# Last feed-forward layer of a two-layer model: merges one block sooner, last group finished in two halves

## The reference

```
x = _layernorm(x + L1_attn(x))            # its output product and gates: "merge" below
# L1_ffn, the last feed-forward part; K0, K1, K2 are matrices of +1 and -1
h = concat([x, -x])                       # 256 features
h = 2 * relu(s0 * h @ K0)                 # 512
h = 2 * relu(s1 * h @ K1)                 # 512
y = s2 * h @ K2                           # 128
out = _layernorm(x + y)                   # (x - mean) / sqrt(var + 1e-5), per row of 128
```

## Time and profile before

| | before |
|---|---|
| device time, three runs | 624.46, 609.24, 624.79 us; median 624.46 |
| profiled execution | 602.81 us, of which the span of the core's instructions is 601.1 |
| granted TensorE clock, mean | 0.986 of 2.4 GHz |
| TensorE busy (products) | 546.1 us, 91% of the span |
| VectorE, ScalarE, GpSimd busy | 407.1, 324.2, 174.4 us |
| last layer | from about 531 us to the end |

### The profile page before, as it was taken

One profiled execution on the slowest core, in us unless ns is written; L12 is line 12 of the kernel. 1 busy time (PEld: TensorE's weight loads), 2 busy tenths in 40 slices (PEclk: granted clock), 3 DMA queues, 4 the chain that ended last, 5 costly groups with the idle time before them and its releaser, 6 DMA issues.

```text
span 601.1 us, 17481 instructions
## 1 busy us (share of the span) xinstructions
PE 546.1 (91%) x7472; PEld 373.3 (62%) x7472; DVE 407.1 (68%) x773; ACT 324.2 (54%) x574; POOL 174.4 (29%) x333
## 2 busy tenths in 40 slices
PE   4799999999999999999999996996999779897993
PEld 2445555555555557777777785774667667565672
DVE  5697999999999826263545337345899871576774
ACT  2327888788888876655555645556422330125441
POOL 7000111445535422010101006246982560010101
PEclk9899999999999999999999999898999999999998
DMA  4778667374240000001000000021673300000011
GB/s 118 153 224 212 190 149 147 81 154 79 57 104 7 5 2 2 0 7 31 1 2 1 0 1 0 2 36 39 124 93 73 73 4 4 5 1 1 1 36 35
DMA packets 54051, 33.82 MB, mean 56 GB/s; under 512 B 38853, under 2 KB 45509, under 8 KB 53974
## 3 DMA queue, kind: packets, MB, share of 16 engines
q1 hardware_dynamic: 48822, 31.65, 23.8%
q10 hardware_dynamic: 5152, 1.05, 1.1%
HBM read 20.83 MB, written 9.44 MB: 50 GB/s over the span
## 4 chain that ended last, share of the span: by engine, by line
PE 70%; DVE 13%; ACT 6%; DMA 6%; issue 2%; SPq 1%; POOL 1%; POOLq 0%; ACTq 0%; DVEq 0%
PE ps L1760 10%; PE ps L1745 9%; PE ps L1512 7%; PE ps L1514 6%; PE ps L1513 6%; PE ps L1860 6%; DMA qst<-shift_sb 4%; PE ps L1724 3%; PE ps L1933 2%; PE ps L2065 2%; DVE filtered L1344 2%; PE ps L2066 2%; ACT prob L682 2%; PE ps L1926 2%; PE ps L1602 1%
## 5 line engine op out<-in xcount | busy, mean ns | idle before, releaser
L1203 DVE TENSOR_REDUCE nmx<-ps 128x1 f32<-128x1024 f32 x128 | 154.1, 1218 | 16.6 <-PE ps L1725 15.2
L682 ACT ACTIVATE prob<-ps 128x512 f32<-128x512 f32 x256 | 137.4, 597 | 26.6 <-PE ps L1745 26.1
L1760 PE MATMUL ps<-prob,vp 128*32 128x128 f32 x2048 | 78.9, 278 | 0.0
L1745 PE MATMUL ps<-qst,kst 50*128 50x512 f32 x256 | 73.6, 492 | 4.7 <-ACT prob L682 3.5
L1760 PEld LDWEIGHTS ps<-prob,vp 128*32 128x32 f32 x2048 | 49.2, 109 | 39.8 <-ACT prob L682 22.4
L1076 DVE TENSOR_TENSOR h_lo<-hf,h_hi 128x512 fp32r<-128x512 f32 x48 | 33.1, 690 | 52.4 <-ACT h_hi L591 50.2
L1512 PE MATMUL ps<-h_hi,w_lo 128*128 128x512 f32 x144 | 58.1, 403 | 2.4 <-DVE h_lo L1076 2.4
L1514 PE MATMUL ps<-h_hi,w_hi 128*128 128x512 f32 x144 | 57.0, 396 | 0.0
L1513 PE MATMUL ps<-h_lo,w_hi 128*128 128x512 f32 x144 | 56.9, 395 | 0.0
L1724 PE MATMUL ps<-kst,qst 48*128 48x512 f32 x128 | 52.6, 412 | 2.2 <-DMA kst<-k_scratch 1.6
L1725 PE MATMUL ps<-kst,qst 48*128 48x512 f32 x128 | 51.5, 404 | 0.0
(11 more groups left out here) (248 smaller groups left out, 1102.3 us busy)
## 6 DMA issues: line engine op xcount, KB each, us to landing
qst<-q_scratch SPq DMA_DIRECT2D x31, 192.0 KB, 4.5
kst<-k_scratch SPq DMA_DIRECT2D x31, 192.0 KB, 4.8
w_raw<-L_ffn_h_w SPq DMA_DIRECT2D x8, 256.0 KB, 3.9
kd<-ka SPq DMA_DIRECT2D x8, 256.0 KB, 6.5
X<-L_attn_x SPq DMA_DIRECT2D x4, 256.0 KB, 5.0
qst<-shift_sb SPq DMA_DIRECT2D x64, 4.0 KB
q_scratch<-w_hi SPq DMA_DIRECT2D x2, 512.0 KB, 5.0
k_scratch<-w_lo SPq DMA_DIRECT2D x2, 512.0 KB, 3.3
```

The source lines that it names most:

```text
L682: nc.scalar.activation(prob[:, n % PROBS, GT * (t % 2):GT * (t % 2) + GT], ps[:, RINGB + i % RING, :], ACT.Exp, scale=SCORE_SCALE).then_in ...
L1203: nc.vector.tensor_reduce(nmx[:, u % 2, j:j + 1], pair, AX.X, ALU.max, negate=True).then_inc(max_done, 1)
L1745: nc.tensor.matmul(ps[:, RINGB + i % RING, :], kst[r:r + 50, p, P * t:P * t + P], half_of(qst[r:r + 50, p, :], u % 2), start=True, stop=Tr ...
L1760: last = nc.tensor.matmul(ps[32 * j:32 * j + 32, PVB, P * half:P * half + P], vp[:, h, t, :], prob[:, n % PROBS, c:c + P], start=(t == 0), ...
```

## The change

Two things are edited, both in the last layer. First, on VectorE and ScalarE the merge steps of the third and fourth group (i = 2 and 3) are put one block earlier among the blocks of the first group. Second, the last group's output product, scaling, transposes, sum, statistics, normalisation and store are done in two halves of 256 rows, each in PSUM banks of its own (`Y5_BANK`, `Y5T_BANK`); the product waits for each low part by itself, and the third group's `stats5` and `norm5` move in between the last group's `rests`.

```diff
--- before.py
+++ after.py
@@ -252,6 +252,7 @@
     xt_hi, xt_lo = x_lo_flat[:, GT:2 * GT], x_lo_flat[:, 2 * GT:3 * GT]
 
     FIR_BANK, UW_BANK, MG_BANK, B_BANK = (0, 4), (4, 0), (0, 4), (4, 0)
+    Y5_BANK, Y5T_BANK = (0, 1), (6, 2)
     OT_BANK, Y4_BANK, X3T_BANK = 2, 3, (2, 1, 1, 1)
 
     with nc.Block() as block:
@@ -507,10 +508,14 @@
                 sp.dma_start(*inverse_of_chunk(1, c)).then_inc(inv_in[1], 16)
 
             out_tiles = out_dram.rearrange("(n p) d -> p n d", p=P)
-            for i, g in enumerate(FINAL):
+            for i, g in enumerate(FINAL[:-1]):
                 sp.wait_ge(out_ready, i + 1)
                 sp.dma_start(out_tiles[:, 4 * g:4 * g + 4, :], X[:, 4 * g:4 * g + 4, :]).then_inc(stored, 16)
-            sp.wait_ge(stored, 16 * GROUPS)
+            for a in range(2):
+                t = 4 * FINAL[-1] + 2 * a
+                sp.wait_ge(out_ready, GROUPS + a)
+                sp.dma_start(out_tiles[:, t:t + 2, :], X[:, t:t + 2, :]).then_inc(stored, 16)
+            sp.wait_ge(stored, 16 * (GROUPS + 1))
 
         def place_u(engine_copy, eng, b, chunks):
 
@@ -817,16 +822,15 @@
             load_oT(0)
             load_oT(1)
             transposed(0)
+            squares(2)
             relus(0, 0, range(FB))
-            squares(2)
-            relus(0, 1, (0,))
             norms_of_o(2)
-            relus(0, 1, (1,))
+            relus(0, 1, (0, 1))
+            squares(3)
             transposed(1)
-            squares(3)
+            norms_of_o(3)
             relus(0, 1, (2,))
             load_oT(2)
-            norms_of_o(3)
             relus(0, 1, (3,))
             relus(1, 0, range(FB))
             scale_y5(0)
@@ -839,7 +843,11 @@
                 relus(i, 1, (2, 3))
                 if i + 1 < GROUPS:
                     relus(i + 1, 0, range(FB))
-                scale_y5(i)
+                    scale_y5(i)
+            act.wait_ge(y5T_psum, GROUPS - 1)
+            for a in range(2):
+                act.wait_ge(y5_psum, GROUPS + a)
+                nc.scalar.activation(y_feat[:, 256 * a:256 * a + 256], ps[:, Y5_BANK[a], 0:256], ACT.Copy, scale=s_out[:, 2:3]).then_inc(y5_scaled, 1)
 
         @block.gpsimd
         def _(pool):
@@ -1037,8 +1045,13 @@
             for i in range(3):
                 rstd(i, stats_ready, mv3, rs3, rstd_ready)
             rstd(3, stats_ready, mv3, rs3, rstd_ready)
-            for i in range(GROUPS):
+            for i in range(GROUPS - 1):
                 rstd(i, stats5_ready, mv4, rs4, rstd5_ready)
+            for a in range(2):
+                r = rs4[:, FINAL[-1], 2 * a:2 * a + 2]
+                pool.wait_ge(stats5_ready, GROUPS + a)
+                link(nc.gpsimd.tensor_scalar(r, mv4[:, FINAL[-1], 2 * a:2 * a + 2, 1], LN_EPS, None, ALU.add))
+                nc.gpsimd.tensor_tensor(r, r, neg_half[:, 0:2], ALU.pow).then_inc(rstd5_ready, 1)
 
         @block.vector
         def _(dve):
@@ -1464,22 +1477,22 @@
             blend_global(2)
             blend_global(3)
             norm3(0)
+            blend_local(2)
             transposed(0)
             add_y4(1)
             stats3(1)
             rests(0, 0, range(FB))
+            sum_squares(2)
             norm3(1)
-            blend_local(2)
             rests(0, 1, (0,))
-            sum_squares(2)
-            rests(0, 1, (1,))
-            transposed(1)
             scale_o(2)
             blend_local(3)
+            rests(0, 1, (1,))
+            sum_squares(3)
+            transposed(1)
             rests(0, 1, (2,))
-            sum_squares(3)
+            scale_o(3)
             rests(0, 1, (3,))
-            scale_o(3)
             add_y4(2)
             rests(1, 0, range(FB))
             stats3(2)
@@ -1487,22 +1500,49 @@
                 add_y5(i - 1)
                 if i == 1:
                     norm3(2)
+                if i == GROUPS - 1:
+                    rests(i, 1, (0,))
+                    stats5(i - 1)
+                    rests(i, 1, (1, 2))
+                    norm5(i - 1)
+                    rests(i, 1, (3,))
+                    continue
                 rests(i, 1, (0, 1))
-                if i + 1 < GROUPS:
-                    transposed(i + 1)
+                transposed(i + 1)
                 rests(i, 1, (2, 3))
                 if i == 1:
                     add_y4(3)
                     stats3(3)
                 stats5(i - 1)
-                if i + 1 < GROUPS:
-                    rests(i + 1, 0, range(FB))
+                rests(i + 1, 0, range(FB))
                 if i == 1:
                     norm3(3)
                 norm5(i - 1)
-            add_y5(GROUPS - 1)
-            stats5(GROUPS - 1)
-            norm5(GROUPS - 1)
+
+            def last_sum(a):
+                t = 4 * FINAL[-1] + 2 * a
+                dve.wait_ge(y5T_psum, GROUPS + a)
+                x2 = X[:, t:t + 2, :].rearrange("p n d -> p (n d)")
+                nc.vector.tensor_tensor(x2, x2, ps[:, Y5T_BANK[a], 0:256], ALU.add).then_inc(y5_added, 1)
+                dve.wait_ge(y5_added, GROUPS + a)
+                for n in range(2):
+                    last = nc.vector.bn_stats(st64[:, FINAL[-1], 2 * a + n, :], X[:, t + n, :])
+                link(last)
+                for n in range(2):
+                    last = nc.vector.bn_aggr(mv4[:, FINAL[-1], 2 * a + n, :], st64[:, FINAL[-1], 2 * a + n, :])
+                last.then_inc(stats5_ready, 1)
+
+            def last_rows(a):
+                dve.wait_ge(rstd5_ready, GROUPS + a)
+                for n in (2 * a, 2 * a + 1):
+                    tile = X[:, 4 * FINAL[-1] + n, :]
+                    last = nc.vector.tensor_scalar(tile, tile, mv4[:, FINAL[-1], n, 0:1], rs4[:, FINAL[-1], n:n + 1], ALU.subtract, ALU.mult)
+                last.then_inc(out_ready, 1)
+
+            last_sum(0)
+            last_sum(1)
+            last_rows(0)
+            last_rows(1)
 
         @block.tensor
         def _(pe):
@@ -2098,12 +2138,29 @@
                 if i + 1 < GROUPS:
                     first(i + 1)
 
-                pe.wait_ge(lo_ready, 8 * i + 8)
-                for k in range(FB):
-                    nc.tensor.matmul(ps[:, 7, :], sw2[:, k, :], h_lo[:, 1, k, :], start=(k == 0), stop=False)
-                    last = nc.tensor.matmul(ps[:, 7, :], sw2[:, k, :], h_hi[:, 1, k, :], start=False, stop=(k == FB - 1))
-                last.then_inc(y5_psum, 1)
-            y_to_tokens(GROUPS - 1)
+                if i + 1 < GROUPS:
+                    pe.wait_ge(lo_ready, 8 * i + 8)
+                    for k in range(FB):
+                        nc.tensor.matmul(ps[:, 7, :], sw2[:, k, :], h_lo[:, 1, k, :], start=(k == 0), stop=False)
+                        last = nc.tensor.matmul(ps[:, 7, :], sw2[:, k, :], h_hi[:, 1, k, :], start=False, stop=(k == FB - 1))
+                    last.then_inc(y5_psum, 1)
+
+            def last_product(a, k):
+                out, cols = ps[:, Y5_BANK[a], 0:256], slice(256 * a, 256 * a + 256)
+                nc.tensor.matmul(out, sw2[:, k, :], h_lo[:, 1, k, cols], start=(k == 0), stop=False)
+                return nc.tensor.matmul(out, sw2[:, k, :], h_hi[:, 1, k, cols], start=False, stop=(k == FB - 1))
+
+            for k in range(FB):
+                pe.wait_ge(lo_ready, 8 * (GROUPS - 1) + FB + k + 1)
+                for a in range(2):
+                    last = last_product(a, k)
+                    if k == FB - 1:
+                        last.then_inc(y5_psum, 1)
+            for a in range(2):
+                pe.wait_ge(y5_scaled, GROUPS + a)
+                for n in range(2):
+                    last = nc.tensor.transpose(ps[:, Y5T_BANK[a], P * n:P * n + P], y_feat[:, 256 * a + P * n:256 * a + P * n + P], ident[:])
+                last.then_inc(y5T_psum, 1)
     last_stage.close()
```

## The result

The changed kernel took 597.03 us in the median of five runs (616.13, 596.84, 597.24, 597.03, 595.94). Two more runs of the kernel before bring its median from 624.46 to 609.24 us (605.62 and 601.33 are new). That is surely faster, and within the 2% that I gave as a measurement's limit.

The account below looks back on a forecast made before the run. TensorE, busy 91% of the span, bounds the kernel, so only its last-layer waits and the tail can be gained: 3.8 + 2.4 = 6.2 us off the 624.46 median gives 618.3, range 597 to 622.

Parts of the forecast that it names:

- Part A: Last layer's first stretch: merges one block sooner remove TensorE's waits of 2.24 and 1.25 us; 3.8 us, lower end 3.0.
- Rival 1: Last layer, first stretch: only the first wait goes, the 1.25 us one stays; total 4.8 us; 0.28 together with rival 2.
- Part B: End of the last layer: last group in halves, third group's statistics and normalisation moved earlier; 2.4 us, ends 1.0 and 3.2.
- The power of two columns: GpSimd, last group's halves: no row for it, bounds 1.04 and 0.52 us; 1.04 taken.
- The 128 KB store: Last group's half store: lands in 2.0 us against 2.3 for 256 KB, so 2.45 from last row to end.
- the second half queued behind the first half's power: GpSimd at the end: second half ready at 593.98 but waiting for the first, so worked 594.26 to 595.61.
- The pitch of 256 columns: TensorE's last output product in halves: 0.12 us taken, bounds 0.11 and 0.24; twelve products end by 590.0.
- rival 2: Last output product: 256 columns cost TensorE full price, 0.24 us each; total 4.8 us; 0.28 together with Rival 1.
- the list of signs: What the trace would show at the end: 8.6 to 9.0 us from last block's `rests` to end instead of 11.7.
- Part A's and B's sum: Both edits in the last layer together: 3.8 + 2.4 = 6.2 us, 1.0% less.
- The range's lower end: Whole kernel: 597 us, from the level of the profiled execution, 602.81 less 6.2.
- part B's own upper bound of 3.2: End of the last layer: 3.2 us saved instead of 2.4 if GpSimd's power of two columns is short.

Follow-up runs that it names:

- the kernel with eleven fillers: The changed kernel with eleven filler products (serving only TensorE's activity) instead of five ahead of the second inputs_of_state: six runs, median 596.80 us.
- the run with the third group alone: The changed kernel with eleven filler products, but the fourth group's merge steps left where they stood before: four runs, median 597.48 us.
- without the fillers: The changed kernel without the five filler products ahead of the second inputs_of_state: all seven runs at 614.77 to 619.70 us.
- the end alone: The kernel before with only the end in two halves (third group's statistics and normalisation moved too), merges as before: 603.17 us, ratio 0.9935.
- the moved steps: The changed kernel with eleven filler products, but the last group finished whole; only the third group's statistics and normalisation stay moved at the end: 602.65 us.

## Why the prediction was right or wrong

**Part A** was right in its steps and its size: 3.9 us for 3.8, which I had called the upper end. In the kernel with eleven fillers `add_y4(2)` ends 0.17 us ahead of TensorE's block (545.58 and 545.75), where I had 0.2 to spare; `norm3(1)` ends 0.87 ahead of the transposes that read it (537.98 and 538.85), where I had 0.9. Rival 1 fell, and the run with the third group alone shows that it was near: there the second wait is 1.23 us, my 1.25, and part A is worth 2.49 us (17.41 less 14.92), my 2.4.

**Part B** was 2.9 for 2.4, two terms mis-sized, both at GpSimd's and the store's end. The power of two columns takes 0.71 and 0.81 us, not the 1.04 of four: my upper bound was taken for the value. With it the second half's rows start 5.93 us after the last low part and not 6.26. The 128 KB store lands in 1.8, not 2.0, and from the last row to the end it is 2.27, not 2.45. Together 0.5. The chain ahead of them was right within 0.2: ScalarE 1.35 us after the last low part's start (I had 1.27), sum 2.35 (2.29), second statistics done 4.69 (4.52). One wait of that chain is gone: I had the second half queued behind the first half's power, but that power ends at 610.29, with VectorE's second statistics, so both let GpSimd go on at 610.37. The pitch of 256 columns is 0.12 (604.77, 604.89), the value I took; rival 2 fell. I also contradicted myself: 2.4 us leave 9.3 us from the last low part to the end, while the list of signs says 8.6 to 9.0.

The Trainium skill's page "DMA: Bandwidth & Descriptors" ("Anatomy of one DMA") gives a DMA a fixed part and its bytes over 436 GB/s, for the path of DMAs that GpSimd issues. By that the half store would be 0.3 us shorter, an estimate; the stores of this kernel, which SyncE issues, differ by 0.5. The Trainium skill's page "TensorE: Matmul & The Clock Gate" (section "The mechanism"; the prediction named the heading behind it) has a weight load overlap products in flight only where the row groups differ. The trace doesn't agree: the products of 256 columns use the whole array, each has a load whose record takes 0.19 us, and they follow one another in 0.12.

**Part A's and B's sum** was therefore 6.9 us for 6.2, and both move the time the way that was said.

**The time itself failed at one step**: "so I take the microseconds off whatever level a run has: 624.46 - 6.2 = 618.3". Taken off the profiled 602.81 the same sum gives 596.6, and the changed kernel's median was 597.03. I read three runs as the kernel's level, although its own profile, at 602.81 with clock 0.986, said what it takes when the clock holds. In the changed kernel the long level is the clock at 0.50 for some 60 us: its profile at 616.13 shows it, and without the fillers all seven runs are at 614.8 to 619.7. For the kernel before that is inferred, as no profile of a run near 624 exists; but its runs at 618 to 626 in the later jobs have a mean clock of 0.924 to 0.942, where those at 599 to 606 have 0.971 to 0.986. As the fall comes ahead of anything the change touches, it was no reason for the changed kernel to be at the upper level more often than at the lower. The range's lower end was drawn too high as well: 596.6 rounded up to 597, with nothing for part B's own upper bound of 3.2 (with that it is 595.8), and the four runs that kept the clock have a median of 596.9.

What stays open: what decides in a given run whether a wait of 1 to 2 us at these gaps brings the clock down. Its length alone doesn't: at the second gap the changed kernel waited 2.01 us in the run of 616.13 and the end alone 1.04 in that of 616.79, where the clock fell, but the changed kernel waited 1.33 in that of 593.76 and the kernel before 0.61 in that of 602.81, where it held. How often it falls differs between jobs. Fourteen runs of the kernel before in these jobs lie between 607 and 616 us, with mean clocks of 0.953 to 0.977; a shorter fall, as in the profile of the moved steps, would explain them, but none of them has a profile.

## What to carry to other kernels

Lay the new order out start to start, with each queue's neighbours, and look for the step with the least to spare; here that gave 3.8 us where 3.9 came, and it named `add_y4(2)` as the next wait. When two paths to the end are nearly equal, shortening one gives nothing (0.05 us for moving all of the third group's steps) until the other is cut as well. And before a time is put to a sum, ask which of the shown runs has the profile that the sum was made from: here a spread of 3% among runs of one program had its cause in the granted clock, and its median was no base to subtract from.

## What the runs showed of the hardware

- With TensorE without a product for 4.92 us ahead of the state's steps, the profile has the clock fall to 0.50 and stay there through those steps, about 60 us of mostly 32 x 32 products with fillers of 512 columns in between; all seven runs were long (mean clock 0.927 to 0.936). It costs 19 us against the kernel with eleven fillers (615.42 and 596.80 in the median). A fall a little earlier, ahead of products of 64 x 64, was over in about 6 us in one profile and sooner in another (0.69 between 478 and 482 us, 1.00 behind).
- The power on GpSimd took 1.04 us for four columns and 0.71 to 0.81 for two.
- Products of 256 columns with a load each follow one another in 0.12 us, half of the 0.234 for 512, although the record of a load is 0.19 us: the load stays hidden.
- ScalarE's scaled copy of 256 columns takes 0.48 us to its reader (606.95 to 607.43 in the chain), and two halves 0.84 together, against 0.69 for 512.
